# A routed transformer block on one core: weight pieces moved in the queue, the job table in the attention block, router products on VectorE

## The chip, the cores and the metric

The kernel runs on one core of one Trainium2 chip. The metric is the device time of one execution in microseconds (us). VectorE, ScalarE, TensorE (PE), GpSimd (POOL) and SyncE (SP) run side by side and meet at semaphores; SP only issues DMAs here.

## The reference, cut to what matters

The input `x` has 16 sequences of 256 tokens of 128 numbers. The block is an attention with 16 heads of 8 numbers and a relative position table, then a mixture of 8 experts with top 2 routing, both gated.

```python
h = layernorm(x) * (1 + ca) + sa
x = x + ga * attention(h)            # scores + Q . rel_emb, softmax, V, Wo
h = layernorm(x) * (1 + cb) + sb
logits = silu(h @ rw1 + rb1) @ rw2 + rb2          # the router: 128 -> 512 -> 8
k_prob, k_index = softmax(top_2(logits))
for e in range(8):                                # every expert 128 -> 512 -> 128
    out += weight_of(e) * (silu(h @ w1[e] + b1[e]) @ w2[e] + b2[e])
x = x + gb * out
```

## The kernel before

The program is a chain of blocks; each ends for all engines before the next begins. `attention` (L162) does attention and routing, `tables` (L1149) makes the table of expert jobs, `experts` (L1268) computes 29 jobs of 384 rows, `combine` (L1487) adds the two results of a token, with gates.

In `attention` a round `b` of 8 steps `p` treats one sequence, two heads a step. The engines' orders are written by hand. A step of VectorE is: `maxima` (L988, four sums of scores and bias with their minimum), copies of a projection from `psM` (`take`, L897), the copy `stage` of the distance products (`put_out`, L942), small routing operations. ScalarE does four exponentials (L570) and two copies `PT` (L581), and Tanh of the router (`squash`, L593). PE makes scores, distances, transposes (L767), values (L782) and projections.

The bias takes a path through memory. VectorE copies the distance products of step n + 6 into one of four `stage` slots, SP writes them to `dist_d` (`write`, L317) and reads them back skewed into `bias` (`read`, L323). The copy into a slot waits until the write of four steps ago has landed (L946). SP's loop (L341) runs six steps ahead of VectorE's.

Beside it one piece of expert weights is prepared a round, 16 in all: SP loads it (`load_piece`, L331), GpSimd splits it in two products (`split_piece`, L393) near the end of its round, SP stores it (`store_piece`, L337). Loop of SP: the store of piece b - 1 and the load of piece b stand ahead of the eight writes and reads of round b.

```python
for b in range(B):
    if b > 0:
        store_piece(b - 1)
    load_piece(b)
    for n in range(PAIRS):
        write(b, n)
```

The routing of a sequence lags by two to five rounds. z is the router's hidden value, th its halved Tanh; `mix` (L441) on GpSimd forms z * tanh(z / 2) in two halves, `th<-z,th`, and the logits follow as two sets of products on PE (L681). GpSimd also makes keys and masks of the top 2 (`keys`, `knock_out`, `count`), the second norm (`normalise_again`, L428), the fp32 splits of Q and K (`stack`, L378), and sends rows with indirect DMAs to `slots_d` (`send`, L480). Five rounds of routing (LAST = 5) run behind the last sequence; I call them the drain.

`tables`: VectorE totals the counts per expert, PE sums them over partitions, VectorE makes `expert` and `firstrow` for 29 jobs in some twenty small operations; SP pads each expert's area with `fill` rows (L1194, eight DMAs, and one at L1190); PE and ScalarE spread the gates to `gbB` (L1228, L1214). In `experts` SP issues weights of two jobs, then waits for sends and fills, then issues `x` (L1327 to L1335). In `combine` ScalarE weights `y1` (L1528), VectorE adds `y2` (L1545) and multiplies by `gbB` (L1550), GpSimd adds `X` (L1558).

Of the kernel before, what the change touches and what calls it, by code (L numbers as in the profile page):

```python
# [8 lines left out]
HID, EXP = 512, 8  # L9
# [89 lines left out]
def program(nc, q, Wq, bq, Wk, bk, Wv, bv, Wo, bo, rel, rw1, rb1, rw2, rb2, w1, b1, w2, b2, c,  # L99
# [3 lines left out]
    with ExitStack() as ctx:  # L103
        def sb(name, shape, dt=FP):
# [20 lines left out]
        ones = sb("ones", [128, 128])  # L125
        slots_d = nc.dram_tensor("slots_d", (UNUSED + ET, ROW), FP, kind="Internal").ap()
        sent = [ctx.enter_context(nc.semaphore(f"sent{k}")) for k in range(RINGS)]
# [9 lines left out]
                  ones, slots_d, sent)  # L137
        mixture(nc, X, ident, modT, pairs_d, b1T, b2T, out_v, v1, v2, earlier, ones, slots_d, sent)
# [23 lines left out]
def attention(nc, x_v, X, ident, modT, mv, rstd, Wq, bq, Wk, bk, Wv, bv, Wo, bo, rel, c, wmod,  # L162
              ahead, rw1_s, rb1T, rw2_s, rb2T, w1, w2, pairs_d, rows, slot_u, v1, v2, earlier, ones,
              slots_d, sent):

    ctx = ExitStack()
    with ctx:
# [82 lines left out]

        def pt(name, shape):
            return ctx.enter_context(nc.psum_tensor(name, shape, FP))
# [8 lines left out]
        def sm(name):  # L261
# [28 lines left out]
            sm("picked"), sm("keyed"), sm("slot_link"), sm("slotted"), sm("moved"))  # L290
        written = [sm(f"written{s}") for s in range(SLOTS)]
        bias_in = [sm(f"bias_in{s}") for s in range(SLOTS)]

        W_DMAS = 1 + 4 + 4 + 1
        block = ctx.enter_context(nc.Block())

        @block.sync
        def _(sp):
# [59 lines left out]
            sp.wait_ge(pair_out, 16 * B)  # L358

        @block.gpsimd  # L360
        def _(pool):
# [44 lines left out]
            for i in range(4):  # L406
# [12 lines left out]
            then(pool.iota(token[:], [[TOKENS, 2], [128, TT]], base=0, channel_multiplier=1,  # L419
                           allow_small_or_imprecise_dtypes=True))  # L420
# [19 lines left out]

            def mix(r, half):  # L441
                pool.wait_ge(squashed, 2 * r + half + 1)
                at = slice(2 * half, 2 * half + 2)
                pool.tensor_tensor(th[:, at, :], z[:, at, :], th[:, at, :], ALU.mult).then_inc(mix_done, 1)  # L444
# [46 lines left out]
            for b in range(B + LAST):  # L491
# [11 lines left out]
                if 0 <= b - 3 < B:  # L503
                    mix(b - 3, 1)
# [28 lines left out]
                if 0 <= b - 2 < B:  # L533
                    fill_rows(b - 2)
                    mix(b - 2, 0)

        @block.scalar
        def _(act):
# [90 lines left out]
            for b in range(B + LAST):  # L629
                if b == 1:  # L630
                    act.wait_ge(taken, 3)
                for p in range(PAIRS):
                    step(b, p)

        @block.tensor
        def _(pe):
# [199 lines left out]
            for b in range(B + LAST):  # L836
                for p in range(PAIRS):
                    step(b, p)

        @block.vector  # L840
        def _(dve):
# [173 lines left out]

            def pick(r, n):
# [36 lines left out]
            def step(b, p):  # L1053
# [40 lines left out]
            for b in range(B + LAST):  # L1094
                for p in range(PAIRS):
                    step(b, p)

# [25 lines left out]
def mixture(nc, X, ident, modT, pairs_d, b1T, b2T, out_v, v1, v2, earlier, ones, slots_d, sent):  # L1123

    with ExitStack() as ctx:
# [8 lines left out]
        p2 = t("p2", [128, TT])  # L1134
        gbB = t("gbB", [128, B, E])
        firstrow = t("firstrow", [128, JOBS], U32)
        expert = t("expert", [128, JOBS], U32)
        fill = t("fill", [128, EK, ROW])
        y = t("y", [128, 2, EK, E])
        row_u = t("row_u", [128, JOBS, EK], U32)  # L1140
        filled = sm("filled")
        y_sent = [sm("y_sent0"), sm("y_sent1")]
        tables(nc, ident, modT, v1, v2, earlier, ones, slots_d, p2, gbB, firstrow, expert, fill, filled)
        experts(nc, ident, slots_d, results_d, pairs_d, b1T, b2T, firstrow, expert, y, row_u, sent,
                filled, y_sent)
        combine(nc, X, results_d, p1, p2, gbB, y_sent, out_v)


def tables(nc, ident, modT, v1, v2, earlier, ones, slots_d, p2, gbB, firstrow, expert, fill, filled):  # L1149

    with ExitStack() as ctx:
        def t(name, shape, dt=FP):
            return ctx.enter_context(nc.sbuf_tensor(name, shape, dt))

        def pt(name, shape):
            return ctx.enter_context(nc.psum_tensor(name, shape, FP))

        def sm(name):
            return ctx.enter_context(nc.semaphore(name))

        gbR = t("gbR", [B, E])
# [424 lines left out]
```

## Time and profile before

| what | value |
|---|---|
| median of 3 runs | 956.13 us (953.19 to 959.73) |
| profiled execution, its own time | 956.31 us |
| its span | 954.5 us |
| PE busy | 647.2 us (68%) |
| VectorE busy | 574.2 us (60%) |
| ScalarE busy | 584.5 us (61%) |
| GpSimd busy | 535.7 us (56%) |

The span is the time from the first to the last instruction in the profile. Busy times of engines overlap. The attention block covers about the first 724 us, the table 730 to 741 us, the experts until 916 us, and the rest is `combine`.

### The profile page before, as it was taken

The page shows a single profiled execution, that of the slowest core. Times are in us where ns is not written, and L with a number is a line of the kernel's source. Part 1 is how long each engine was busy: PE and PEld are TensorE (multiplying, and loading weights), DVE is VectorE, ACT ScalarE, POOL GpSimd, SP SyncE. Part 2 cuts the span into 40 slices and gives each one's busy share as a digit, 9 for nine tenths or more (in the row PEclk, how much of TensorE's full clock was granted, in tenths as well). Part 3 has the DMA queues.
Part 4 walks back from the last instruction along what each step waited for, and adds up shares of the span by engine and source line. Part 5 has one row for each costly group of instructions (what it writes and reads, how often), then busy time and mean ns, then how long its engine had stood idle before and what let it go on. Part 6 is the DMA issues. An engine that isn't in the chain of part 4 may idle for free. (4 is left out here: it accounts for less than half of the span.)

```text
span 954.5 us, 18251 instructions
## 1 busy us (share of the span) xinstructions
PE 647.2 (68%) x4994; PEld 482.9 (51%) x4994; DVE 574.2 (60%) x2030; ACT 584.5 (61%) x1714; POOL 535.7 (56%) x821
## 2 busy tenths in 40 slices
PE   4678777877658585857658585857423499999900
PEld 3455555654436354534436354534213499899800
DVE  5878877765747584755747584754211166566517
ACT  2278887766647584846647584857101388888713
POOL 2545545848567484848567484836773045556534
PEclk9579999989788897979788897979665599999965
DMA  6766976581936547382836547391002588888627
GB/s 194 236 159 205 279 236 198 164 265 62 282 99 212 166 144 225 97 267 64 276 103 207 166 145 227 95 289 60 14 20 78 163 250 275 270 274 274 215 70 194
DMA packets 189433, 172.27 MB, mean 180 GB/s; under 512 B 18115, under 2 KB 175588, under 8 KB 189334
## 3 DMA queue, kind: packets, MB, share of 16 engines
q1 hardware_dynamic: 184070, 162.54, 55.8%
q0 software_dynamic: 4832, 8.44, 2.5%
q8 instruction: 42, 0.69, 0.3%
q14 instruction: 57, 0.47, 0.2%
q10 hardware_dynamic: 432, 0.14, 0.1%
HBM read 97.94 MB, written 74.63 MB: 181 GB/s over the span
## 5 line engine op out<-in xcount | busy, mean ns | idle before, releaser
L570 ACT ACTIVATE P<-NS,nmax 128x256 f32<-128x256 f32 x512 | 254.2, 499 | 162.9 <-DVE nmax L996 150.5
L947 DVE COPY stage<-psDist 128x768 f32<-128x768 f32 x125 | 119.3, 954 | 159.1 <-DMA dist_d<-stage 107.2
L996 DVE CUSTOM_DVE_ANT_0 NS<-psS,bias 128x256 f32<-128x256 f32 x512 | 185.5, 418 | 10.4 <-issue 8.4
L749 PE MATMUL psS<-Kst,Qst 32*128 32x256 f32 x512 | 69.5, 352 | 139.1 <-DVE nmax L996 138.9
L767 PE MATMUL psT<-ident,P 128*128 128x128 f32 x1024 | 147.6, 289 | 12.8 <-ACT PT L581 10.6
L581 ACT ACTIVATE PT<-psT 128x512 f32<-128x512 f32 x256 | 137.6, 582 | 20.8 <-PE psT L767 18.8
L767 PEld LDWEIGHTS psT<-ident,P 128*128 128x128 f32 x1024 | 126.0, 150 | 38.0 <-issue 25.9
L1349 POOL DMA_INDIRECT results_d<-y,row_u x87 | 86.1, 990 | 98.9 <-ACT y L1368 80.6
L749 PEld LDWEIGHTS psS<-Kst,Qst 32*128 32x128 f32 x512 | 41.6, 200 | 167.1 <-DVE nmax L996 156.3
L444 POOL TENSOR_TENSOR th<-z,th 128x512 f32<-128x512 f32 x32 | 40.7, 1273 | 145.9 <-ACT th L596 145.9
L570 ACT ACTIVATION_READ_ACCUMULATOR P<-NS,nmax 128x1 f32 x512 | 96.6, 189 | 0.0
L1466 DVE TENSOR_TENSOR FL<-F,FH 128x384 fp32r<-128x384 f32 x116 | 61.9, 554 | 52.2 <-ACT FH L1382 41.6
L690 PE MATMUL psM<-hT,Wqk 128*128 128x256 f32 x244 | 82.5, 469 | 1.3 <-DVE xqk L918 1.3
L782 PE MATMUL psO<-PT,V 128*32 128x256 f32 x1024 | 80.8, 440 | 0.8 <-ACT PT L581 0.8
L1374 ACT ACTIVATE F<-psH,b1T 128x384 f32<-128x384 f32 x116 | 66.2, 584 | 19.9 <-PE psH L1425 19.3
L486 POOL DMA_INDIRECT slots_d<-rows,slot_u x64 | 63.9, 998 | 22.9 <-issue 22.9
L383 POOL TENSOR_TENSOR part<-xqk,lowQ 128x512 fp32r<-128x512 f32 x32 | 33.4, 1042 | 62.4 <-DVE xqk L918 54.7
L918 DVE TENSOR_SCALAR xqk<-psM,bqk 128x256 f32<-128x256 f32 x122 | 53.2, 478 | 15.7 <-PE psM L690 15.7
L755 PE MATMUL psDist<-Tst,Qst 32*128 32x192 f32 x488 | 61.6, 333 | 0.0
L690 PEld LDWEIGHTS psM<-hT,Wqk 128*128 128x128 f32 x244 | 49.7, 226 | 22.6 <-issue 10.9
L1382 ACT ACTIVATE FH<-F 128x384 fp32r<-128x384 f32 x116 | 58.2, 532 | 0.0
L1423 PE MATMUL psH<-xH,wUp 128*128 128x384 f32 x116 | 45.1, 389 | 2.7 <-DVE xL L1459 1.5
(231 smaller groups left out, 1378.7 us busy)
## 6 DMA issues: line engine op xcount, KB each, us to landing
dist_d<-stage SPq DMA_DIRECT2D x128, 384.0 KB, 4.0
bias<-dist_d SPq DMA_DIRECT2D x256, 192.0 KB, 3.3
wUp<-pairs_d SPq DMA_DIRECT2D x29, 512.0 KB
wDown<-pairs_d SPq DMA_DIRECT2D x29, 512.0 KB
pairs_d<-pair SPq DMA_DIRECT2D x16, 512.0 KB, 3.1
x<-slots_d SPq DMA_DIRECT2D x29, 193.5 KB
raw<-in_L_ffn_w_dram SPq DMA_DIRECT2D x16, 256.0 KB, 3.7
y<-results_d SPq DMA_DIRECT2D x16, 256.0 KB, 4.9
```

Source lines behind the costliest of these rows:

```text
L486: pool.indirect_dma_start(out=slots_d, out_offset=bass.IndirectOffsetOnAxis(ap=slot_u[:, j, n:n + 1], axis=0), in_=rows[:, j, r % RINGS, k ...
L570: act.activation(P[:, p % 2, h, q, :], NS[:, p % 2, h, q, :], ACT.Exp, scale=-1.0, bias=nmax[:, p % 2, k:k + 1], accum_out=lsum[:, b % 2, ...
L581: act.activation(PT[:, (p // 2) % 2, 2 * (p % 2) + h, :], psT[:, h, :], ACT.Copy)\
L690: mm = pe.matmul(bank[:, S * n:S * n + S], w[:, 128 * g:128 * g + 128], hT[:], start=True, stop=True)
L749: mm = pe.matmul(psS[:, h, S * q:S * q + S], Qst[at, b % 2, g, 128 * q:128 * q + 128], Kst[at, b % 2, g, :], start=True, stop=True)
L767: mm = pe.transpose(psT[:, h, S * k + 128 * q:S * k + 128 * q + 128], P[:, p % 2, h, q, 128 * k:128 * k + 128], ident[:])
L782: mm = pe.matmul(psO[32 * a:32 * a + 32, 0:S], V[:, par, k, g, a, :, :].rearrange("p c d -> p (c d)"), PT[:, g % 2, a, S * k:S * k + S], s ...
L947: dve.tensor_copy(stage[:, p % STAGES, :, :, :], bank[:, :, 0:2 * RW].rearrange("p h (q c) -> p h q c", q=2)).then_inc(dist_out, 1)
L996: dve.tensor_tensor_reduce(NS[:, p % 2, h, q, :], psS[:, h, S * q:S * q + S], bias[:, p, h, q, :], 1.0, 3e38, ALU.add, ALU.min, nmax[:, p ...
L1349: pool.indirect_dma_start(out=results_d, out_offset=bass.IndirectOffsetOnAxis(ap=row_u[:, j, k:k + 1], axis=0), in_=y[:, j % 2, k, :], in_ ...
L1374: act.activation(F[:, k, :], psH[:, k % 2, 0:ET], ACT.Silu, bias=b1T[:, bass.ds(e, 1), k:k + 1].rearrange("p a k -> p (a k)"))\
L1466: dve.tensor_tensor(FL[:, j % 2, k, :], F[:, k, :], FH[:, j % 2, k, :].bitcast(FP), ALU.subtract)\
```

## The change

It has four parts.

1. SP's store of piece b - 1 and load of piece b are issued ahead of write 4 of round b instead of write 0.
2. The block `tables` is gone. Its constants are made by GpSimd ahead of the rounds; counts and job table are computed by VectorE and PE at the end of the attention block, behind the last `earlier`; the fills are issued there by SP (one, and four experts) and ScalarE (four experts). In `experts` SP waits for sends and fills first and issues `x` of job 0, its up weights, `x` of job 1, then the rest.
3. The gates' rows `gbB` are made in `combine`, by PE and ScalarE ahead of the weighting of `y1`.
4. `mix` moves from GpSimd to VectorE, into steps 0 and 1 of the round after its Tanh began.

```diff
             for b in range(B):
-                if b > 0:
-                    store_piece(b - 1)
-                load_piece(b)
                 for n in range(PAIRS):
+                    if n == 4:
+                        if b > 0:
+                            store_piece(b - 1)
+                        load_piece(b)
                     write(b, n)
...
             sp.wait_ge(pair_out, 16 * B)
+            sp.wait_ge(consts_done, 1)
+            sp.dma_start(slots_d[UNUSED:UNUSED + ET, :].rearrange("(p k) e -> p k e", p=128),
+                         fill[:]).then_inc(filled, 16)
+            pad(sp, range(EXP // 2))
...
+        def pad(engine, experts):
+            engine.wait_ge(table, 1)
+            for x in experts:
+                n = engine.value_load(cnt_u[0:1, x:x + 1], min_val=0, max_val=TOKENS)
+                engine.dma_start(slots_d[bass.ds(n + AREA * x, ET), :].rearrange("(p k) e -> p k e", p=128),
+                                 fill[:]).then_inc(filled, 16)
...
@@ GpSimd, its rounds @@
-                if 0 <= b - 3 < B:
-                    mix(b - 3, 1)
...
-                    mix(b - 2, 0)
...
@@ ScalarE, behind its rounds @@
+            pad(act, range(EXP // 2, EXP))
...
@@ VectorE, a step @@
+                if 0 <= b - 3 < B and p < 2:
+                    mix(b - 3, p)
                 if routed and p in (1, 2):
                     pick(route_r, p)
...
@@ VectorE, behind its rounds @@
+            dve.wait_ge(keyed, 4 * B)
+            dve.tensor_tensor(total[:], earlier[:, TT, :], earlier[:, 0, :], ALU.subtract).then_inc(totalled, 1)
...
+            dve.tensor_copy(firstrow[:], first_f[:])
...
@@ SP, experts @@
-            for j in range(2):
-                load_w(j, 0, wUp, up, 0, up_in)
-            load_w(0, 1, wDown, down, 0, down_in)
             for k in range(RINGS):
                 sp.wait_ge(sent[k], 16 * 4 * B // RINGS)
             sp.wait_ge(filled, 16 * (EXP + 1))
-            for j in range(2):
-                load_x(j)
-            load_w(1, 1, wDown, down, 0, down_in)
+            load_x(0)
+            load_w(0, 0, wUp, up, 0, up_in)
+            load_x(1)
+            load_w(0, 1, wDown, down, 0, down_in)
+            for n, w, arrived in ((0, wUp, up_in), (1, wDown, down_in)):
+                load_w(1, n, w, up, 0, arrived)
...
@@ ScalarE, combine @@
             act.activation(p2[:], p2[:], ACT.Exp).then_inc(probs, 1)
+            act.wait_ge(gates_turned, 1)
+            act.activation(gbR[:], psL[0:B, 0:E], ACT.Copy).then_inc(gates_out, 1)
+            for g in range(B * E // 512):
+                act.wait_ge(gate_rows, g + 1)
+                act.activation(gbB[:, 4 * g:4 * g + 4, :].rearrange("p b e -> p (b e)"),
+                               psG[:, g % 2, :], ACT.Copy).then_inc(gates_wide, 1)
             act.wait_ge(probs, 4)
```

SP's queue at the turn to round 2 before: `dist_d<-stage` is a write, `bias<-dist_d` the two reads of the step before, and the write behind `raw` is write 0 of round 2.

```order
L329 DMA bias<-dist_d 128x2x192 x2
L339 DMA pairs_d<-pair 128x1024
L335 DMA raw<-in_L_ffn_w_dram 128x512
L320 DMA dist_d<-stage 128x4x192
L329 DMA bias<-dist_d 128x2x192 x2
L320 DMA dist_d<-stage 128x4x192
L329 DMA bias<-dist_d 128x2x192 x2
```

The same place now; the first write here is write 0 of round 2 and the one behind `raw` is write 4.

```order
L349 DMA dist_d<-stage 128x4x192
L358 DMA bias<-dist_d 128x2x192 x2
L349 DMA dist_d<-stage 128x4x192
L358 DMA bias<-dist_d 128x2x192 x2
L349 DMA dist_d<-stage 128x4x192
L358 DMA bias<-dist_d 128x2x192 x2
L349 DMA dist_d<-stage 128x4x192
L358 DMA bias<-dist_d 128x2x192 x2
L368 DMA pairs_d<-pair 128x1024
L364 DMA raw<-in_L_ffn_w_dram 128x512
L349 DMA dist_d<-stage 128x4x192
L358 DMA bias<-dist_d 128x2x192 x2
```

Four writes and four pairs of reads now stand ahead of the store of `pair` and the load of `raw`.

GpSimd in round 5 before, from the split of the weight piece to the second split of Q in the next round (`part`, `Qst`):

```order
L398 TENSOR_TENSOR pair<-raw,pair 128x512
L476 COPY rows<-rows 128x2x128
L477 COPY rows<-token 128x2x2
L444 TENSOR_TENSOR th<-z,th 128x512
L450 TENSOR_SCALAR key<-logit,v 128x8 x2
L453 TENSOR_TENSOR key<-key,order 128x16
L383 TENSOR_TENSOR part<-xqk,lowQ 128x512
L385 TENSOR_TENSOR Qst<-xqk,part 128x512
L425 COPY linvD<-linv 128x256
L444 TENSOR_TENSOR th<-z,th 128x512
L383 TENSOR_TENSOR part<-xqk,lowQ 128x512
L385 TENSOR_TENSOR Qst<-xqk,part 128x512
```

And now, from the same place of a round:

```order
L432 TENSOR_TENSOR pair<-raw,pair 128x512
L514 COPY rows<-rows 128x2x128
L515 COPY rows<-token 128x2x2
L488 TENSOR_SCALAR key<-logit,v 128x8 x2
L491 TENSOR_TENSOR key<-key,order 128x16
L417 TENSOR_TENSOR part<-xqk,lowQ 128x512
L419 TENSOR_TENSOR Qst<-xqk,part 128x512
L468 COPY linvD<-linv 128x256
L417 TENSOR_TENSOR part<-xqk,lowQ 128x512
L419 TENSOR_TENSOR Qst<-xqk,part 128x512
L496 TENSOR_SCALAR chosen<-key,kmax 128x8 x2
```

Both operations `th<-z,th` are gone from it. On VectorE the end of step 0 of round 6 and the start of step 1 stood thus before (`v` and `slot_f` are routing, the ISA row is a maximum of step 1):

```order
L1020 TENSOR_REDUCE v<-logit 128x2
L1038 TENSOR_REDUCE slot_f<-slot_c 128x4
L918 TENSOR_SCALAR xqk<-psM,bqk 128x256 x2
L1004 RECIPROCAL linv<-lsum 128x32
L947 COPY stage<-psDist 128x768
L996 ISA NS,nmax<-psS,bias 128x256
```

And now:

```order
L1063 TENSOR_REDUCE v<-logit 128x2
L1081 TENSOR_REDUCE slot_f<-slot_c 128x4
L956 TENSOR_SCALAR xqk<-psM,bqk 128x256 x2
L1042 RECIPROCAL linv<-lsum 128x32
L985 COPY stage<-psDist 128x768
L1057 TENSOR_TENSOR th<-z,th 128x512
L1034 ISA NS,nmax<-psS,bias 128x256
```

Step 0 now holds one `th<-z,th` between its `stage` copy and the maxima of step 1. The second stands in the same place of step 1, there also ahead of `kmax<-key`.

## Rows read from the trace of the kernel before

**Rows 1.** Table of waits, last row SP's queue (us in total, times, longest)

```profile
DVE stage L947 <- DMA dist_d<-stage: 107.5, 15, 9.9
...
DVE kmax L1020 <- POOL key L453: 25.2, 16, 4.6
...
DVE stage L947 <- PE psDist L698: 10.4, 13, 1.1
...
SPq L339 <- POOL pair L398: 265.6, 16, 21.0
```

**Rows 2.** Timeline of SP's queue, a store; page, writes of `stage` (us to landing)

```profile
579.02 0.35 SPq L339 DMA_DIRECT2D pairs_d<-pair  x1
...
dist_d<-stage SPq DMA_DIRECT2D x128, 384.0 KB, 4.0
```

**Rows 3.** Timeline of GpSimd, end of a round and the next one's products

```profile
577.73 1.26 POOL L398 TENSOR_TENSOR pair<-raw,pair 128x512 fp32r<-128x512 f32 x1
...
589.99 1.28 POOL L444 TENSOR_TENSOR th<-z,th 128x512 f32<-128x512 f32 x1 [10.52 <-ACT th L596]
...
596.67 1.27 POOL L444 TENSOR_TENSOR th<-z,th 128x512 f32<-128x512 f32 x1
```

**Rows 4.** Timeline of VectorE, three copies of `stage`, two with the wait

```profile
583.95 0.96 DVE L947 COPY stage<-psDist 128x768 f32<-128x768 f32 x1 [9.44 <-DMA dist_d<-stage]
...
595.26 0.96 DVE L947 COPY stage<-psDist 128x768 f32<-128x768 f32 x1 [1.10 <-issue]
...
626.66 0.96 DVE L947 COPY stage<-psDist 128x768 f32<-128x768 f32 x1 [7.86 <-DMA dist_d<-stage]
```

**Rows 5.** Stretches: us, busy PE, PEld, DVE, ACT, POOL, then PEclk, DMA, GB/s

```profile
93.50:123.60 30.10, 23.88 (x248) 16.25 (x248) 25.12 (x95) 27.12 (x91) 16.18 (x22) 1.00 0.77 237
...
579.00:620.70 41.70, 28.96 (x252) 20.25 (x252) 26.72 (x103) 26.72 (x85) 25.87 (x43) 0.84 0.57 177
```

**Rows 6.** Timeline of VectorE, copies of `stage` in an early round

```profile
98.45 0.96 DVE L947 COPY stage<-psDist 128x768 f32<-128x768 f32 x1 [1.91 <-DMA dist_d<-stage]
...
105.93 0.96 DVE L947 COPY stage<-psDist 128x768 f32<-128x768 f32 x1
```

**Rows 7.** Timeline of PE, transposes of P in the round of rows 4

```profile
592.77 1.91 PE L767 MATMUL psT<-ident,P 128*128 128x128 f32 x8
...
596.02 1.04 PE L767 MATMUL psT<-ident,P 128*128 128x128 f32 x8
```

**Rows 8.** Timelines of GpSimd and SP's queue, end of the attention block

```profile
723.49 0.96 POOL L486 DMA_INDIRECT slots_d<-rows,slot_u  x1 [0.30 <-issue]
730.03 0.42 POOL L1199 IOTA steps<- 128x88 f32 x1 [5.58 <-POOLq L167]
...
732.65 8.44 SPq L1194 DMA_DIRECT2D slots_d<-fill  x8
...
746.01 1.44 SPq L1318 DMA_DIRECT2D x<-slots_d  x2
```

**Rows 9.** Timeline of ScalarE, gates' copies and start of the last block

```profile
731.13 0.27 ACT L1211 ACTIVATE gbR<-psL 16x128 f32<-16x128 f32 x1 [35.95 <-PE psL L1221]
...
738.67 0.60 ACT L1214 ACTIVATE gbB<-psG 128x512 f32<-128x512 f32 x1 [1.11 <-PE psG L1228]
...
924.94 0.23 ACT L1522 ACTIVATE p<-p 128x32 f32<-128x32 f32 x1
927.52 1.28 ACT L1528 ACTIVATE y<-y,p 128x128 f32<-128x128 f32 x4 [2.35 <-DMA y<-results_d]
```

**Rows 10.** Timelines of VectorE and GpSimd, two chunks of the last block

```profile
928.91 1.14 DVE L1545 SCALAR_TENSOR_TENSOR y<-y,p 128x128 f32<-128x128 f32 x4 [2.92 <-ACT y L1528]
930.09 0.69 DVE L1550 TENSOR_TENSOR y<-y,gbB 128x512 f32<-128x512 f32 x1
...
933.71 2.15 DVE L1545 SCALAR_TENSOR_TENSOR y<-y,p 128x128 f32<-128x128 f32 x4
...
933.87 1.31 POOL L1558 TENSOR_TENSOR y<-y,X 128x512 f32<-128x512 f32 x1 [1.74 <-DVE y L1550]
```

More of the change, by code:

```diff
@@ L136, in program @@
                   ahead, rw1_s, rb1T, rw2_s, rb2T, w1, w2, pairs_d, rows, slot_u, v1, v2, earlier,
[L137 to L138 removed]
+                  ones, slots_d, sent, p2, firstrow, expert, fill, filled)
+        mixture(nc, X, ident, modT, pairs_d, b1T, b2T, out_v, slots_d, sent, p2, firstrow, expert, filled)
 def past(engine, semaphore, count):
@@ L249, in attention @@
         lower = t("lower", [128, 128])
+        steps = t("steps", [128, EXP, MOST])
+        until = t("until", [128, EXP, EXP])
+        total = t("total", [128, EXP])
+        cnt = t("cnt", [128, EXP])
+        cnt_u = t("cnt_u", [128, EXP], U32)
+        more = t("more", [128, EXP, MOST])
+        wide = t("wide", [128, EXP, EXP])
+        ntile = t("ntile", [128, EXP])
+        cum = t("cum", [128, EXP])
+        jobno = t("jobno", [128, JOBS])
+        gone = t("gone", [128, JOBS, EXP])
+        gone_t = t("gone_t", [128, JOBS, EXP])
+        ex = t("ex", [128, JOBS])
+        first_f = t("first_f", [128, JOBS])
         def pt(name, shape):
@@ L418, in _ @@
                       allow_small_or_imprecise_dtypes=True)
-            then(pool.iota(token[:], [[TOKENS, 2], [128, TT]], base=0, channel_multiplier=1,
-                           allow_small_or_imprecise_dtypes=True))
+            pool.iota(steps[:], [[0, EXP], [ET, MOST]], base=0, channel_multiplier=0,
+                      allow_small_or_imprecise_dtypes=True)
+            pool.iota(until[:], [[1, EXP], [-1, EXP]], base=0, channel_multiplier=0,
+                      allow_small_or_imprecise_dtypes=True)
+            pool.iota(jobno[:], [[1, JOBS]], base=0, channel_multiplier=0,
+                      allow_small_or_imprecise_dtypes=True)
+            pool.memset(fill[:, :, 0:E], 0.0)
+            pool.memset(fill[:, :, E:ROW], float(NO_ROW))
+            pool.iota(token[:], [[TOKENS, 2], [128, TT]], base=0, channel_multiplier=1,
+                      allow_small_or_imprecise_dtypes=True).then_inc(consts_done, 1)
+            pool.wait_ge(consts_done, 1)
             def widen(b):
@@ L838, in _ @@
                     step(b, p)
+            pe.wait_ge(totalled, 1)
+            pe.matmul(psM[:, 0:EXP], ones[:], total[:], start=True, stop=True).then_inc(counted, 1)
         @block.vector
@@ L1120, in newton, with mixture @@
     then(dve.tensor_tensor(r, r, tmp, ALU.mult))
-def mixture(nc, X, ident, modT, pairs_d, b1T, b2T, out_v, v1, v2, earlier, ones, slots_d, sent):
+def mixture(nc, X, ident, modT, pairs_d, b1T, b2T, out_v, slots_d, sent, p2, firstrow, expert, filled):
     with ExitStack() as ctx:
@@ L1497, in combine @@
         y2 = t("y2", [128, TT, E])
+        gbR = t("gbR", [B, E])
+        gbB = t("gbB", [128, B, E])
+        psG = ctx.enter_context(nc.psum_tensor("psG", [128, 2, 512], FP))
+        psL = ctx.enter_context(nc.psum_tensor("psL", [128, 512], FP))
         loaded = [sm(f"loaded{c}") for c in range(CHUNKS)]
@@ L1529, in _ @@
                 i.then_inc(weighted, 1)
+        @block.tensor
+        def _(pe):
+            pe.transpose(psL[0:B, 0:E], modT[:, 5, :], ident[:]).then_inc(gates_turned, 1)
+            pe.wait_ge(gates_out, 1)
+            for g in range(B * E // 512):
+                past(pe, gates_wide, g - 1)
+                for k in range(4):
+                    b = 4 * g + k
+                    mm = pe.matmul(psG[:, g % 2, 128 * k:128 * k + 128],
+                                   ident[0:B, b:b + 1].broadcast_to([B, 128]), gbR[:],
+                                   start=True, stop=True)
+                mm.then_inc(gate_rows, 1)
         @block.vector
```

154 lines of the change are left out of this document (37 added, 117 removed).

## Prediction

> **What bounds the kernel now.** I read the table of waits first, then the engines' timelines of one attention round, then the place where attention hands over to the experts. The chain that ended last holds only the final 31 us and says nothing of the loop. The table of waits names one pair that explains the rest: VectorE's `stage` copy waits 107.5 us in 15 waits for a DMA of `stage`, and the SP queue waits 265.6 us in 16 waits for GpSimd's `pair` [rows 1]. One such wait is up to 21.0 us long; it ends at 579.02, when SP can issue the store of `pair` [rows 2]. The write of `dist_d` that the next round needs stands behind that store. GpSimd makes the piece last in its round, behind four indirect DMAs, and ends it at 577.73 + 1.28 = 579.0 [rows 3]. Four `stage` slots later VectorE has none free and stops for 9.44 us; in the next round it is 7.86 us [rows 4].
>
> A round is 626.66 - 583.95 = 42.71 us from stalled copy to stalled copy [rows 4]. No engine fills it: in 41.7 us PE is busy 28.96, VectorE and ScalarE 26.72 each, GpSimd 25.87, the DMAs 0.57 [rows 5]. An early round, before routing starts and with a stall of 1.9 us only, took 30.1 us with ScalarE at 27.12. So the floor of a round is some 28 us, and the wait for `pair` is the bound.
>
> The stall has a second price. The two steps behind it take 595.26 - 583.95 = 11.31 us; the same two steps early in the run take 105.93 - 98.45 = 7.48 us [rows 4, 6]. In them eight transposes of PE take 1.91 us, and 1.04 us once the clock is back [rows 7]; the granted clock of the later round is 0.84 as a mean, of the early one 1.00 [rows 5]. PE stood idle, its clock fell to 1.2 GHz, and the steps that follow are run at that level.
>
> **The pieces moved in SP's round.** Nothing is added: 16 stores and 16 loads stay. The store of piece b-1 and the load of piece b go from ahead of write 0 to ahead of write 4. SP runs six steps ahead of VectorE, so write 4 is asked for in the seventh step of the round before (p = 6, the row at 583.95 would be that copy, at 574.5 without its wait). GpSimd's piece is done at 579.0, and two 1.27 us products less, at about 577. The write then is held some 3 us. Its slot is asked for again only four steps later, 14 us, and a write lands in 4.0 us [rows 2]: about 6 us in hand. Hence I cost the wait at nothing, and take off all 107.5 us. If this cover were gone, each microsecond of GpSimd past it would come back in about 13 rounds.
>
> The clock: of the 3.8 us between 11.31 and 7.48 us part is work that the early round had not (the router's two copies to `z`, routing). I estimate three fifths of it, 2.3 us, as returned for each of the ten full stalls, and 5 us for the four small ones together: 28 us. The bounds are 0 (PE idles enough elsewhere) and 14 x 3.8 = 53.
>
> **Products by VectorE.** GpSimd loses 32 products of 1.27 us, 2.5 us a round [rows 3]. VectorE gains them, in steps 0 and 1. It has run no such product, so it is bounded: the nearest row is its product of two SBUF tensors of 128x512, 0.69 us, about 0.61 from start to start. The upper bound is in the same rows: four small operations with two SBUF inputs take 1.14 us alone and 2.15 us when a product of GpSimd of 1.30 us runs in them [rows 10]. So VectorE can stand for the rest of GpSimd's operation, up to 0.61 + 1.27 = 1.9 us; in steps 0 and 1 GpSimd works nearly without a break. I take 1.2 us each: 26 products in full rounds make 31 us, bounds 16 and 49. Against it stand waits of VectorE that go when GpSimd is 1.27 us earlier and VectorE 2.4 us later: for `key` 25.2 us in all, of which I give half to the full rounds, and 10.4 us for the turned rows (L698) [rows 1]. I take off 22 us, leaving +9, with ends -6 and +38.
>
> The Trainium skill ("SBUF — State Buffer", section "SBUF: two separate sides") says that VectorE with two SBUF inputs and GpSimd take a shared pair of ports as an exclusive lock for a whole instruction, the later one blocking fully. That speaks against this edit; the 1.01 us added in rows 10 agree. Without the rule the products would be 16 us gross and the sum 15 us lower.
>
> **The drain.** Behind the last full round GpSimd is the pacer, by its timeline without a gap over long stretches. Six products fall into it, 6 x 1.24 = 7.4 us. VectorE is idle there and its price hides behind GpSimd's other work: -7, bounds 0 and -10.
>
> **The job table.** Before: GpSimd's last send starts at 723.49 and the next block's first instruction at 730.03; SP's eight fills run from 732.65 to 741.1, weights are issued first, and `x` at 746.01 [rows 8]. From 730.03 to 741.1 table and fills took 11 us; with four of the eight fills, of 1.06 us each, on idle ScalarE, 6.8 us. They can begin at the last count, behind which GpSimd still has eight sends of 1.27 us, 10 us: they are covered. The block's end stays, 730.03 - 724.45 = 5.6 us. So `x` is issued near 730.7 instead of 746.01: -15.3, and it no longer shares the DMAs with 1.5 MB of weights, so I say -15.5. Ends: -12 (up weights late) and -19. The constants that GpSimd adds stand ahead of round 0, where it waits; each is at most like the `steps` of 0.42 us [rows 8], five of them under 2 us: 0.
>
> **The gates.** They move to the last block. There PE's 32 passes and ScalarE's copies stand ahead of the weighting of `y1`. From the copy `gbR` at 731.13 to the end of the last `gbB` copy at 739.27 it is 8.1 us. ScalarE is free for `gbR` at 925.2, so it starts `y1` at 933.3, not 927.5: 5.8 us later [rows 9]. A first gap of VectorE between its chunks closes, some 0.6 us: +5, with ends 0 (PE at 2.4 GHz) and +6. Nothing hides it, as VectorE's chunks set the end from there.
>
> **The sum**, against the profiled execution's 956.3 us (span 954.5; the median of the runs, 956.1, is the same): -107.5 - 28 + 9 - 7 - 15.5 + 5 = -144, so 812 us. A round becomes 42.7 - 9.6 - 2.3 + 0.7 = 31.5 us, just above ScalarE's 26.7 and VectorE's 26.7 + 1.3.
>
> **The rivals.**
> - Better: the steps close up to ScalarE's work. The early round, without its stall of 1.9 us, took 28.2 us with 27.12 us of ScalarE's work [rows 5, 6]. A round of 29.5 us instead of 31.5, in 13 rounds, gives 786. Against it: in steps 2 to 4 VectorE waits for short chains through GpSimd and PE. 0.15.
> - The clock does not come back, since PE still has gaps, or VectorE's products open new ones: the 28 us stay, 840. For it: the clock was also below 1.00 in rounds with stalls of 2 to 4 us. Against: the early round at 1.00. 0.10.
> - The wait takes another place: GpSimd sets the round or its piece comes too late for write 4. Its work of 25.87 us, less 2.5 us, is under the new round; were it late by 4 us beyond the cover, 13 x 4 = 52 us come back: 864. 0.07.
> - The move does nothing: `pair` is last in GpSimd's order, and SP stands at it anyway. Then only table, drain and gates count: 956 - 18 = 938. Against: the distance of 14 us above. 0.03.
> - Slower than before: VectorE, in order, stands at each product until Tanh is done, and Tanh stands behind ScalarE's gather, which needs PE, which needs VectorE's maxima. The place is steps 0 and 1 of each round. It decides from 144 / 26 = 5.5 us a product; at 6 us the time is 969. In the trace GpSimd's first product starts at 589.99, just as Tanh ends, and the second has its Tanh by 596.67 [rows 3]; VectorE's places are behind the copies of 595.26 [rows 4] and of the next step, 6 and 2 us later. 0.02.
>
> **How the numbers follow.** The forecast has 0.63. Its own range is 797 to 828. To leave out no more than two in ten I take in the better case in part and the lost clock: 788 to 842. A measurement of this kernel tells about 1%, 10 us, from no change. Every case but the last lies over 1% below 956, and I keep 0.01 for the middle: faster 0.97, same 0.01, slower 0.02.
>
> **What would show it.** The wait of `stage` for its DMA should be gone from the table, SP's wait for `pair` be short or harmless, and the copies of a round 31 to 32 us apart, with transposes of 1.04 us in every step. The granted clock of the rounds should be near 1.00. The product on VectorE should measure 0.7 to 1.9 us. Fills should start before GpSimd's last send, the first `x` be issued 6 us behind it, and `y1` begin 9 to 10 us into the last block. A copy that still waits for its write, transposes of 1.9 us every round, or VectorE idle before its product would prove a step wrong.

## The result, and the profile after

The changed kernel takes 811.64 us (median of 4 runs, 810.99 to 816.91) where the kernel before took 956.36 us beside it (4 runs, 953.19 to 959.73). The ratio is 0.8498, with a 95% interval of 0.8452 to 0.8545. The predicted time was 812, in a range of 788 to 842. The sum came out, but several of its terms were off, in both directions, and their errors cancel; the experiments below show which.

The profiled execution has a span of 809.2 us, 145.3 less than before. First the table of waits, in the columns of [rows 1]; the last three rows are SP's queue.

```profile
DVE kmax L1063 <- POOL key L491: 19.5, 15, 4.6
...
DVE stage L985 <- PE psDist L741: 13.5, 14, 1.6
...
SPq L349 <- DVE stage L985: 142.6, 81, 12.6
SPq L368 <- POOL pair L432: 61.0, 11, 12.0
SPq L358 <- DMA dist_d<-stage: 56.1, 54, 2.1
```

The row of 107.5 us, `stage` for its DMA, is gone. SP still stands at GpSimd's `pair`, but for 61.0 us instead of 265.6, and it now waits for VectorE's `stage`, which is the right way round. `kmax` still waits for `key`: 19.5 of the 25.2 us have stayed.

The copies of `stage` in one round, from VectorE's timeline. The two rows of [rows 4] with 9.44 and 7.86 us of waiting answer to the row at 466.80.

```profile
442.77 0.89 DVE L985 COPY stage<-psDist 128x768 f32<-128x768 f32 x1
446.43 0.95 DVE L985 COPY stage<-psDist 128x768 f32<-128x768 f32 x1
450.27 0.94 DVE L985 COPY stage<-psDist 128x768 f32<-128x768 f32 x1
454.55 0.96 DVE L985 COPY stage<-psDist 128x768 f32<-128x768 f32 x1 [0.77 <-PE psDist L734]
...
466.80 0.96 DVE L985 COPY stage<-psDist 128x768 f32<-128x768 f32 x1 [0.93 <-PE psDist L741]
```

The next round's first copy is at 474.17, so a round is 31.4 us; nine rounds agree to 0.1 us. The same stretch of both kernels, in the columns of [rows 5], before and then after:

```profile
595.26:637.90 42.64, 28.23 (x256) 19.52 (x255) 27.38 (x105) 27.21 (x88) 25.65 (x43) 0.88 0.57 178
```

```profile
442.77:474.17 31.40, 26.11 (x255) 18.38 (x256) 27.55 (x107) 26.80 (x88) 25.18 (x43) 1.00 0.77 237
```

The work is the same but for PE's, which runs 2.1 us shorter at a granted clock of 1.00. What left is idle time of all engines. Where SP's queue met GpSimd's piece, now in the middle of the round ([rows 2, 3] before):

```profile
437.71 1.28 POOL L432 TENSOR_TENSOR pair<-raw,pair 128x512 fp32r<-128x512 f32 x1
```

```profile
439.01 0.35 SPq L368 DMA_DIRECT2D pairs_d<-pair  x1
439.40 0.43 SPq L364 DMA_DIRECT2D raw<-in_L_ffn_w_dram  x1
439.94 0.84 SPq L349 DMA_DIRECT2D dist_d<-stage  x1
```

The store still follows the piece at once, and the write of `dist_d` still stands behind it; but VectorE wants that slot only at 450.27, 10.3 us later. It is the slot that the copy at 435.41 had filled, four copies before.

At the hand-over to the experts, timelines of GpSimd, SP's queue and PE ([rows 8] before):

```profile
580.75 1.06 POOL L524 DMA_INDIRECT slots_d<-rows,slot_u  x1 [0.51 <-issue]
...
589.70 0.96 POOL L524 DMA_INDIRECT slots_d<-rows,slot_u  x1 [0.30 <-issue]
```

```profile
584.07 4.22 SPq L321 DMA_DIRECT2D slots_d<-fill  x4
597.66 0.37 SPq L1262 DMA_DIRECT2D x<-slots_d  x1
```

```profile
602.52 0.69 PE L1367 MATMUL psH<-xH,wUp 128*128 128x384 f32 x1 [1.58 <-DMA wUp<-pairs_d]
```

Four fills run beside the sends (four more on ScalarE's queue), and `x` is issued 7.0 us behind the end of the last send, 590.66. Before it was 746.01 - 724.45 = 21.6 us. In the last block ScalarE's timeline is now ([rows 9] before):

```profile
774.41 0.25 ACT L1474 ACTIVATE gbR<-psL 16x128 f32<-16x128 f32 x1
776.82 0.60 ACT L1477 ACTIVATE gbB<-psG 128x512 f32<-128x512 f32 x1 [2.16 <-PE psG L1495]
...
781.94 0.60 ACT L1477 ACTIVATE gbB<-psG 128x512 f32<-128x512 f32 x1 [1.11 <-PE psG L1495]
782.43 3.89 ACT L1484 ACTIVATE y<-y,p 128x128 f32<-128x128 f32 x13
```

The 145.3 us of the span by place: up to the last maxima of sequence 15 it is 658.06 against 526.18, -131.9. The drain to the end of the last send is 66.4 against 64.5, -1.9. From there to the first product of job 0 it is 28.15 against 11.86, -16.3. The experts differ by 0.6, and the last block is 30.85 against 36.22, +5.4.

### The profile page after: what moved, and what is told of

Its sections match the earlier page's. It is cut to its first block and busy times, and to the rows that moved or that the text cites. A ratio compares the mean times of both kernels' runs of the same rounds, so it can differ in the third digit from the quotient of the medians.

```text
span 809.2 us, 18250 instructions
## 1 busy us (share of the span) xinstructions
PE 608.3 (75%) x4994; PEld 458.0 (57%) x4994; DVE 588.2 (73%) x2062; ACT 578.2 (71%) x1714; POOL 505.2 (62%) x789
## 5 line engine op out<-in xcount | busy, mean ns | idle before, releaser
L803 PE MATMUL psT<-ident,P 128*128 128x128 f32 x1024 | 137.5, 277 | 8.7 <-ACT PT L616 7.9
L803 PEld LDWEIGHTS psT<-ident,P 128*128 128x128 f32 x1024 | 117.0, 143 | 29.5 <-issue 13.3
L785 PE MATMUL psS<-Kst,Qst 32*128 32x256 f32 x512 | 65.4, 334 | 50.4 <-DVE nmax L1034 50.3
L1410 DVE TENSOR_TENSOR FL<-F,FH 128x384 fp32r<-128x384 f32 x116 | 61.8, 554 | 52.5 <-ACT FH L1326 52.4
L785 PEld LDWEIGHTS psS<-Kst,Qst 32*128 32x128 f32 x512 | 38.7, 187 | 78.0 <-DVE nmax L1034 70.0
L726 PE MATMUL psM<-hT,Wqk 128*128 128x256 f32 x244 | 71.6, 419 | 5.2 <-DVE xqk L956 4.1
L818 PE MATMUL psO<-PT,V 128*32 128x256 f32 x1024 | 70.2, 393 | 0.8 <-ACT PT L616 0.8
L791 PE MATMUL psDist<-Tst,Qst 32*128 32x192 f32 x488 | 57.8, 315 | 0.0
L726 PEld LDWEIGHTS psM<-hT,Wqk 128*128 128x128 f32 x244 | 44.1, 201 | 21.6 <-DVE xqk L956 11.1
L419 POOL TENSOR_TENSOR Qst<-xqk,part 128x512 fp32r<-128x512 f32 x32 | 48.7, 1522 | 2.5
L488 POOL TENSOR_SCALAR key<-logit,v 128x8 f32<-128x8 f32 x64 | 21.1, 340 | 44.0 <-DVE v L1063 44.0
```

The source lines that it names most:

```text
L726: mm = pe.matmul(bank[:, S * n:S * n + S], w[:, 128 * g:128 * g + 128], hT[:], start=True, stop=True)
L785: mm = pe.matmul(psS[:, h, S * q:S * q + S], Qst[at, b % 2, g, 128 * q:128 * q + 128], Kst[at, b % 2, g, :], start=True, stop=True)
L803: mm = pe.transpose(psT[:, h, S * k + 128 * q:S * k + 128 * q + 128], P[:, p % 2, h, q, 128 * k:128 * k + 128], ident[:])
L818: mm = pe.matmul(psO[32 * a:32 * a + 32, 0:S], V[:, par, k, g, a, :, :].rearrange("p c d -> p (c d)"), PT[:, g % 2, a, S * k:S * k + S], s ...
L1410: dve.tensor_tensor(FL[:, j % 2, k, :], F[:, k, :], FH[:, j % 2, k, :].bitcast(FP), ALU.subtract)\
```

## The experiments

Each is an edit of the kernel before (b_...) or of the one after (a_...). I compare ratios to the kernel before; 0.001 is about 1 us.

**b_pieces: the pieces moved, and nothing else.**

```diff
 # before
-                if b > 0:
-                    store_piece(b - 1)
-                load_piece(b)
                 for n in range(PAIRS):
+                    if n == 4:
+                        if b > 0:
+                            store_piece(b - 1)
+                        load_piece(b)
                     write(b, n)
```

> The kernel before, with only the store and the load of the weight pieces moved ahead of write 4. Theory of the prediction: the wait goes (-107.5 us) and the clock comes back (-28 us), so 956 - 135 = 821 us. What the trace of the changed kernel says: its attention rounds end 131.9 us earlier although the products on VectorE lengthen steps 0 and 1 by 0.95 us a round, 12 us in 13 rounds; so this edit alone should give 956 - 144 = 812 us, with rounds of 30.5 us. Rival (GpSimd, which still has its 2.5 us of products a round, sets the round or brings the piece too late): 825 us or more, with a wait of the copies for their write left in the table.

824.08 us (823.46 to 825.71), ratio 0.8606, 0.8581 to 0.8632. Of 144 us the move alone brings 133. The prediction's 821 us is within 3 us of it; the 812 us that I had read out of the changed kernel's trace are not. I had taken rounds of 30.5 us, without any price for the products; they are 31.3 us, as short as those of the full change, with the products still on GpSimd. The reason stands in the timelines of VectorE and GpSimd of this kernel:

```profile
413.09 1.14 DVE L1042 CAST slot_u<-slot_f 128x4 uint32<-128x4 f32 x1
```

```profile
412.93 1.28 POOL L445 TENSOR_TENSOR th<-z,th 128x512 f32<-128x512 f32 x1
```

VectorE's cast of four numbers a partition takes 1.14 us under GpSimd's product, and in the kernel after, where the product is gone from there, 0.15 us. It ends 0.02 us behind the product. In the kernel before, where the product was on GpSimd too, the two did not meet like this: the cast took 0.16 to 0.52 us in the rounds. The groups of the cast, in the kernel before and then in b_pieces (us in all, mean ns of one):

```profile
L1041 DVE CAST slot_u<-slot_f 128x4 uint32<-128x4 f32 x16 | 5.0, 312 | 0.1
```

```profile
L1042 DVE CAST slot_u<-slot_f 128x4 uint32<-128x4 f32 x16 | 14.5, 904 | 0.1
```

So it is the shorter round that brings them together.

**a_mixpool: the products back on GpSimd.** The kernel after with `mix` as in before.

```diff
 # after: GpSimd's step, behind widen(b - 1) and fill_rows(b - 2); VectorE's mix removed
+                if 0 <= b - 3 < B:
+                    mix(b - 3, 1)
...
+                    mix(b - 2, 0)
```

> The changed kernel with the router's products back on GpSimd, in their old places. Theory A (prediction, products cost VectorE 31 us and save 22 us of its waits in full rounds, and 7 us in the drain): 811.6 - 2 = 810 us. Theory B (trace: the products cost 0.95 us a round and cover nothing, the drain gains 1.9 us by them): 811.6 - 12.4 + 1.9 = 801 us. Theory C (GpSimd at 27.7 us of work in a round of 30.5 us comes late with keys and norms): 812 us or more.

815.95 us (814.12 to 818.7), ratio 0.8521, 0.8496 to 0.8546; rounds 31.3 us. Theory B, 801 us, is out. Theory C has the number but not the reason: GpSimd does not come later with `key` (the wait of `kmax` is 1.2 us a round, as in the kernel after), and the cast takes 1.15 us again in all but one of the full rounds. Step 0, with the cast in it, is 4.03 us long; in the one round in which the two miss each other (cast 0.19 us) it is 3.07 us. Products on VectorE gain some 2 us in all, though the interval of the change's ratio takes in no gain too, and none in the rounds.

**a_nomix: VectorE's products cut to one column.** The rest of Tanh goes unmultiplied into the logits, so the routing and the output are not the reference's.

```diff
 # after
-                dve.tensor_tensor(th[:, at, :], z[:, at, :], th[:, at, :], ALU.mult).then_inc(mix_done, 1)
+                dve.tensor_tensor(th[:, at, 0:1], z[:, at, 0:1], th[:, at, 0:1], ALU.mult).then_inc(mix_done, 1)
```

> The kernel after, with the router's products cut to one column of each of the two tokens' halves (the rest of the router's tanh enters the logits unmultiplied, so the routing differs): it leaves out 32 products of 0.69 us on VectorE and nothing else. Theory A: the products cost the round what the copies' distances show, 0.6 + 0.35 us in steps 0 and 1, and the wait for key does not shrink with them: 12 rounds by 0.95 us, about 800 us. Rival B: each also holds VectorE's next operations (the whole 1.2 us that I had taken): 12 x 2.4, about 785 us. Rival C: something else takes up the time at once, 808 to 812 us. The number of rows per expert may differ and shift the experts by a few microseconds; the rounds are read from the trace for that reason.

799.15 us (796.05 to 801.83), ratio 0.8354, 0.8324 to 0.8384; rounds 30.5 us. Theory A: the 512 columns cost 0.9 us a round, 0.45 us each, over the cut operations that stay. Those take 0.07 and 0.20 us from start to start in steps 0 and 1, so by an estimate the whole products cost at most 1.2 us a round. `kmax` waits 19.5 us for `key`, as with them, so they hid nothing and were hidden by nothing there. GpSimd's groups of `Qst`, with the products (after) and without (a_nomix):

```profile
L419 POOL TENSOR_TENSOR Qst<-xqk,part 128x512 fp32r<-128x512 f32 x32 | 48.7, 1522 | 2.5
```

```profile
L419 POOL TENSOR_TENSOR Qst<-xqk,part 128x512 fp32r<-128x512 f32 x32 | 40.9, 1278 | 2.5
```

The product of VectorE lengthens GpSimd's operation that it meets by 0.24 us as a mean over all 32.

**a_keys: GpSimd's `keys` ahead of its norm.**

```diff
 # after, GpSimd's step
+                if 0 <= b - 4 < B:
+                    keys(b - 4, 1)
                 if b < B - 2:
...
-                if 0 <= b - 4 < B:
-                    keys(b - 4, 1)
```

> The kernel after, with GpSimd's tile `keys` of block b-4 issued ahead of its `normalise` of block b+2 in the step in which VectorE's kmax waits for key. Theory A: the wait of 1.18 us a round lies on the path that sets the round, so the rounds go from 31.4 to about 30.5 us: 12 rounds by 0.9 to 1.2 us, 797 to 801 us. Rival B: TensorE or ScalarE takes up the round (26.1 and 26.8 us busy of 31.4), or th comes late to its users instead: 808 to 815 us.

806.95 us (804.97 to 810.27), ratio 0.8414, 0.8389 to 0.8439: 8 us better than the change, where theory A wanted 11 to 15. Rounds are 30.6 us. VectorE's timeline, after and then a_keys, shows where the rest of the 1.19 us stays:

```profile
458.52 0.17 DVE L1063 TENSOR_REDUCE kmax<-key 128x2 f32<-128x16 f32 x1 [1.19 <-POOL key L491]
...
459.52 0.95 DVE L985 COPY stage<-psDist 128x768 f32<-128x768 f32 x1
```

```profile
452.96 0.17 DVE L1063 TENSOR_REDUCE kmax<-key 128x2 f32<-128x16 f32 x1
...
454.52 0.96 DVE L985 COPY stage<-psDist 128x768 f32<-128x768 f32 x1 [0.48 <-PE psDist L737]
```

A wait of 0.48 us for PE, which the first had covered, comes out. The profiled execution, 810.27 us, is the slowest of the six. It had lost 2.8 us before the full rounds (its copy of step 0 is at 163.00, against 160.18 after), the ten rounds from there bring 7.8, so that the copy at 469.17 is 5.0 us ahead of 474.17, and 2.9 of these are lost by the last send, which starts at 587.64 instead of 589.70.

**a_n2 and a_n6: another place for the pieces.**

```diff
 # after
-                    if n == 4:
+                    if n == 2:     # a_n2; n == 6 in a_n6
```

> The changed kernel with store and load ahead of write 2 instead of write 4. Theory (the cover is the distance in steps between GpSimd's piece and the first copy that needs the slot): the queue stands at the store two steps longer, 7.5 us, of which 6 us were in hand, so each of some 11 full rounds waits again 1 to 2.5 us: 811.6 + 20 = 832 us, range 822 to 842. Rival (the wait was one of order alone, any place behind write 0 does): 812 us. Rival (the clock falls with any stall, and its price comes back whole): 832 + 11 x 3 = 865 us.

840.92 us (839.91 to 842.01), ratio 0.8782, 0.8756 to 0.8807: 9 us above the theory's 832, at the upper end of its range (822 to 842). The wait of `stage` for its DMA is back, and SP waits longer for `pair`:

```profile
DVE stage L985 <- DMA dist_d<-stage: 17.8, 11, 3.6
```

```profile
SPq L368 <- POOL pair L432: 141.9, 16, 13.1
```

> The kernel after, with the pieces ahead of the seventh write of the round instead of the fifth. Theory A: what counts is that the pieces are in the queue before the write that waits longest and land before the stage copy; with write 6 they start some 7 to 8 us later than with write 4, and land about as late as the stage copy wants them: the wait stage <- DMA comes back with 0 to 3 us a round, 812 to 845 us. Rival B: any place ahead of the last write will do, 810 to 814 us.

813.62 us (813.44 to 815.15), ratio 0.8496, 0.8463 to 0.8528: equal to the change. No wait of `stage` for its DMA is in its table, so theory A's reason, that a later transfer comes too late, falls. Of the three places tried, 4 and 6 are equal, and at 2 GpSimd's piece is too late.

**a_table: job table and gates alone.** The kernel after with the pieces and the products as before.

```diff
 # after, and the edit of a_mixpool
                 for n in range(PAIRS):
-                    if n == 4: ...
                     write(b, n)
 # store_piece(b - 1) and load_piece(b) stand ahead of the loop again
```

> The kernel after, with the pieces back behind the loop's last write (as before) and the router's products back on GpSimd: what is left is the job table inside the last block, and the gates' inputs there. Forecast from the trace of after: -16.3 us between the last send and the first product of job 0, +5.4 us in the last block, and the clock as before: 956 - 11 = 945 us (941 to 949). Rival: the table's gain hung on the sends that the moved pieces had brought forward; then it is within 3 us of before.

948.69 us (947.77 to 951.71), ratio 0.9897, 0.9859 to 0.9934: 9.9 us. The last send ends at 728.54 and `x` is issued at 735.91, 7.4 us behind it, with the rounds as before. So this gain doesn't hang on the move. Together with b_pieces' 133.3 us it makes 143.2; the kernel with both (a_mixpool) gains 141.4.

**a_gates: ScalarE's copies of the gates between its weightings.**

```diff
 # after, ScalarE in combine
-            for g in range(B * E // 512): ... gbB copies, all four
             for c in range(CHUNKS):
+                if c % 2 == 0: ... the gbB copy of g = c // 2
```

> The changed kernel with ScalarE's copies of the gates' rows put between the weightings: the copy of group g ahead of chunks 2g and 2g+1 instead of all four ahead of chunk 0. Theory (the gates' copies delay the first weighting from 777.4 to 782.4 us and nothing hides them): the last block ends 4.5 to 5 us earlier, 811.6 - 5 = 807 us. Rival (VectorE's first product with the gates or the loads of y set the start): 811 us or more.

809.34 us (808.38 to 812.37), ratio 0.8458, 0.8435 to 0.8482. That is 4 us less than the change, with overlapping intervals; the trace is clearer. From its start the last block takes 31.2 us instead of 36.2. From `gbR` to the first weighting it takes 2.97 us instead of 8.02:

```profile
776.88 0.25 ACT L1474 ACTIVATE gbR<-psL 16x128 f32<-16x128 f32 x1
779.36 0.60 ACT L1480 ACTIVATE gbB<-psG 128x512 f32<-128x512 f32 x1 [2.23 <-PE psG L1496]
779.85 1.26 ACT L1485 ACTIVATE y<-y,p 128x128 f32<-128x128 f32 x4
```

**a_both: a_keys and a_gates together.**

> The kernel after with both edits, the keys ahead of the norm (a_keys: ratio 0.841) and ScalarE's copies of the gates between the weightings (a_gates: 0.846, after: 0.850). They lie in different blocks, so the gains add: ratio 0.837, about 802 us. Rival: the gates' gain is within the scatter and the ratio stays at 0.841, 806 us.

800.51 us (798.75 to 802.34), ratio 0.8358, 0.8332 to 0.8384. It is the best version with the right output, about 13 us under the change, and the two gains (8 and 4) add.

**b_busy, b_full, b_fit: is it the clock?** TensorE gets products of zeros to do in the step in which VectorE waits.

```diff
 # before, PE's step, behind the turned products
+                if p == 7 and 5 <= b < B - 1:          # 4 <= b in b_busy
+                    for _ in range(21):                # 14 in b_busy, 42 in b_full
+                        pe.matmul(psO[:, 0:S], zeros[:], Wqk[...], start=False, stop=False)
```

> The kernel before, with 14 products of zeros (128x256) added to psO's sums in the step in which TensorE waits for the stage copy (blocks 4 to 14), so that TensorE has work while VectorE waits for the pieces; results unchanged. Theory A: the two steps behind the wait are long in the kernel before (5.5 and 5.2 us where they take 3.6 and 3.8 after the change) because TensorE had stood still and its clock was down; then they shorten by 3.3 us a round at ten rounds, 33 us, and the time is about 923 us. Rival B: they are long because the pieces' burst ends beneath them; then nothing is gained, 956 us or a little more. Rival C: the added products themselves delay the step's real ones by up to 2 us a round, above 965 us.

956.82 us (952.02 to 961.32), ratio 0.998, 0.9952 to 1.0008. No gain. But in the ten full stalls the products left 4.2 to 5.1 us of the gap empty, and the second step behind it still took 3.9 to 6.4 us, where it takes 3.1 to 3.6 in the kernel after; behind a gap of 4.20 us the eight transposes took 1.91 us, as in [rows 7]. The clock had fallen all the same. One smaller stall does put the question, in block 4: 5.94 us of waiting, in which the 14 products kept TensorE at work up to the next scores. In b_fit below the same place has no added products, a stall of 5.96 us, and TensorE idle for 5.99 us. The two steps behind the stall, in the columns of [rows 5], b_busy and then b_fit:

```profile
204.96:212.33 7.37, 7.26 (x62) 5.38 (x62) 7.36 (x30) 5.61 (x20) 1.93 (x4) 1.00 0.94 279
```

```profile
204.90:214.84 9.94, 7.23 (x49) 4.94 (x50) 7.54 (x31) 6.61 (x22) 2.68 (x5) 0.66 0.93 282
```

The stall is the same and so is the DMA's load (0.94 and 0.93), so rival B, the pieces' burst, does not explain the difference. With the clock up the two steps take 7.37 us, as in the kernel after; with the clock down they take 2.57 us more.

> The kernel before, with 42 products of zeros (128x256) added to psO's sums in the step with the stall, in blocks 5 to 14, so that TensorE works through nearly all of it (42 x 0.22 = 9.3 us of a gap of 10.4 us; in b_busy 14 products had filled 6 us counted at half clock, left 4.2 us empty, and the two steps behind stayed long). Theory A: the steps behind the stall are long because TensorE's clock fell in the gap; with no gap of more than 1 to 2 us they take 7.4 us instead of 10.7, ten rounds by 3.3 us, about 925 us. Rival B: what makes them long is not the clock: 956 us or more.

1012.8 us (1010.49 to 1017.43), ratio 1.0561, 1.0525 to 1.0597. I had taken one product for 0.22 us; it is 0.44, so they ran on into the next step and held it up by 7 us. The clock's part can be read beside that: the transposes behind the gap took 1.04 us, the second step behind it 3.6 us in nine rounds and 3.1 in the tenth, and the stretch 380 to 480 us has a granted clock of 1.00.

> As b_full, with 21 products of zeros instead of 42. In b_full each took 0.44 us, two passes of 0.22, and not 0.22, so they ran 8 us past the wait; TensorE's granted clock stayed at full level from 224 us on and the second step behind the stall took 3.6 us instead of 5.2. 21 products fill 9.2 us of the gap of 10.4. Theory A: the clock alone is what the two steps want: both come to 3.8 and 3.6 us, a round from 42.7 to 39.4 us, ten rounds by 3.3, about 925 us (920 to 932). Rival B: only the second step shortens, 1.6 us a round: 940 us. Rival C: with the steps shorter the piece's transfer is asked for sooner relative to the loop and the stall grows by as much: 950 to 957 us.

941.68 us (938.75 to 952.24), ratio 0.982, 0.9773 to 0.9868. It gains 17 us by added work, between theory A (925) and no gain, near rival B's 940. Its profiled execution was the slowest of its runs, 952.24 us, and shows both outcomes side by side. PE's timeline of two rounds, with the products filling both gaps:

```profile
368.21 9.23 PE L817 MATMUL psO<-Wqk,zeros 128*128 128x256 f32 x42
378.67 0.38 PE L749 MATMUL psS<-Kst,Qst 32*128 32x256 f32 x2 [1.22 <-DVE nmax L1000]
...
382.51 1.81 PE L767 MATMUL psT<-ident,P 128*128 128x128 f32 x8
...
409.63 9.23 PE L817 MATMUL psO<-Wqk,zeros 128*128 128x256 f32 x42
419.96 0.39 PE L749 MATMUL psS<-Kst,Qst 32*128 32x256 f32 x2 [1.10 <-DVE nmax L1000]
...
422.91 1.04 PE L767 MATMUL psT<-ident,P 128*128 128x128 f32 x8
```

In the first the clock still falls to 1.2 GHz for a few microseconds, and the two steps behind the stall take 4.3 + 5.1 us; in the second it stays at 2.4 GHz and they take 4.4 + 3.6 us. It stayed in four rounds of ten, with the stall unchanged (its step takes 12.8 us in the first and 12.6 us in the second). So what shortens the second step is the clock. The first step keeps 4.2 to 5.1 us even in the four rounds, against 3.8 after: behind a full stall VectorE's maxima wait 0.4 to 1.2 us there, for something that the profile does not name. That wait stands in the kernel before too (0.6 us as a mean of the ten full rounds), and not in the kernel after. So not all of 33 us is the clock's; the best run, 938.75 us, gained 19.

## Why the prediction was right, and where its terms were off

**The pieces moved.** Right in its cause; the closeness is luck. I had 107.5 us for the stall and 28 for the clock, 135.5; b_pieces measures 133.3. The distances of the copies of `stage` in b_pieces and in the kernel before take the 133 apart. The steps with the stall give 96 us: over the ten full rounds 8.8 us each and not 9.6, for a wait of 0.93 us for PE (the row at 466.80) had stood beneath it. The two steps behind the stall give 47 us and not 28, 34 of them in the ten full rounds. And step 0, in which the cast now meets GpSimd's product, takes 8 us back, for which I had no term. Errors of 12, 19 and 8 us cancel nearly. The cover that I worked out, 6 us for write 4, held (10.3 us from the write at 439.94 to the copy at 450.27, less 4 us to land), and a_n2 shows its edge: two writes earlier, 27 us come back. A reading of mine was off by a little: the wait that ends at 579.02 is 20.4 us long; the one of 21.0 us is in another round.

**The clock.** The term "2.3 us of 3.8, ten times" was too small, and it lumped two things. The two steps behind the stall went from 10.7 to 7.3 us as a mean of ten rounds, 3.4 us a round. Of these 0.6 us is the maxima's wait, which had no place in the sum. What is left for the clock is about 2.8 us, an estimate by difference; the pair of b_busy and b_fit measures 2.57 us. The 5 us for the four small stalls were too small as well: the two steps behind them gave 10 us. The last 3 of the 47 us are in a round ahead of the first of these stalls and belong to neither. The case in which the clock doesn't return is excluded by the row of 442.77 to 474.17 at 1.00, and b_fit shows the price apart from the stall.

**Products by VectorE.** The sum +9 was wrong in both its parts. I took 1.2 us each, 31 us in full rounds; a_nomix shows 0.45 us each on the path, 12 us for these 26 (at most 16 us with what its cut operations still take) and 14 us in all 32. And I took off 22 us for waits of VectorE that would go; in the full rounds `kmax` kept its 1.18 us each time, and the 5.7 us that it lost are in the drain. The true other side was one that I had not looked for: with the pieces moved and the products left on GpSimd, VectorE's cast `slot_u` meets a product and loses 1.0 us a round. Taken and given back, the rounds are equal (31.3 and 31.4 us), and with the drain it is -2.2 us where I had +9 - 7 = +2.

My sum without the ports had the products at 16 us gross, and that is nearer to the measured 12 to 16. The rows at 443.58 to 443.81 show why: it is VectorE that comes first, with 0.69 us, and GpSimd that is held up.

```profile
443.58 0.69 DVE L1057 TENSOR_TENSOR th<-z,th 128x512 f32<-128x512 f32 x1
```

```profile
443.81 1.60 POOL L419 TENSOR_TENSOR Qst<-xqk,part 128x512 fp32r<-128x512 f32 x1
```

The Trainium skill ("SBUF — State Buffer", section "SBUF: two separate sides") says that whichever of the two starts first holds the pair of ports for its whole instruction and that the other blocks. The trace agrees in kind: `Qst` takes 0.32 us more than its 1.28 in a_nomix, while the two overlap for 0.46 us. What I had wrong is who pays: I had charged it to VectorE alone.

**The drain.** I took GpSimd's 7.4 us of products off and said that VectorE's price hides behind GpSimd's other work. It doesn't: -1.9, where a_nomix, with the products cut on VectorE too, has -4.6 (61.8 us). VectorE's timeline and GpSimd's, in the drain of the kernel after:

```profile
529.28 0.69 DVE L1057 TENSOR_TENSOR th<-z,th 128x512 f32<-128x512 f32 x1 [0.97 <-ACT th L631]
...
530.76 0.69 DVE L1057 TENSOR_TENSOR th<-z,th 128x512 f32<-128x512 f32 x1 [0.71 <-ACT th L631]
531.37 0.16 DVE L1063 TENSOR_REDUCE kmax<-key 128x2 f32<-128x16 f32 x1
```

```profile
531.71 0.59 POOL L496 TENSOR_SCALAR chosen<-key,kmax 128x8 f32<-128x8 f32 x2 [2.45 <-DVE kmax L1063]
```

VectorE stands at each product until Tanh is done, `kmax` stands behind both, and GpSimd waits 2.45 us for it. It is the mechanism of my "slower" rival, in the one place where nothing else lies between the products.

**The job table.** I had -15.5 and it is -16.3. `x` was to be issued 6 us behind the last send's end and is issued 7.0 behind it, -14.6; from there to the first product it is 4.9 us instead of 6.6, although that product now waits 1.58 us for its up weights, as the range's upper end had it.

**The gates.** +5 predicted, +5.4 measured. Table and gates together: -10.5 predicted, -9.9 in a_table.

**The sum.** -135.5 against -133.3, -10.5 against -9.9, and +2 against -2.2: by group the errors are 2, 1 and 4 us. Within the first and the last they are larger and cancel, up to 19 us against 12 and 8, so the range was earned by the mechanism and the hit at 812 is partly luck. The "better" rival asked for rounds of 29.5 us. The way there was named against it, short chains through GpSimd and PE, and a_keys opens one of them by moving one call, for 0.8 us a round.

## What to carry to other kernels

Before moving a DMA in an engine's queue, find which instruction stands behind the one that waits, and count how long it is until someone needs that instruction's result: here a store that still waits costs nothing, as 10 us lie between the write behind it and its user. What a stall gives back when it goes is its own length less the waits beneath it, plus the slower steps that TensorE runs behind it, less what newly collides once the rounds are shorter. When an operation goes from one engine to another, look on both for what overlaps it in time, for what it would meet in the new timing if it stayed, and at the places where the pipeline is nearly empty, since there it waits in front of others.

## What the hardware showed that I had not expected

A cast of 128x4 numbers on VectorE took 1.14 us under a GpSimd product of 1.28 us, and 0.15 us without it: a very small operation can cost as much as a large one. In the kernel before, with the same two operations, it took at most 0.52 us in the rounds; the collision came with the shorter round. The other way, VectorE's product of 0.69 us made GpSimd's operation 0.32 us longer. A stall of 5.9 us with TensorE kept at work left no trace in the two steps behind it, 7.37 us at a granted clock of 1.00; with TensorE idle they took 9.94 us at 0.66. And TensorE's clock did not fall at each gap alike: in b_fit, with 21 products filling it, what was left of the gap, 1.04 to 1.93 us, was followed by 2.4 GHz in four rounds, and 1.22 to 1.99 us by 1.2 GHz in six. What decides between them stays open.
